# A graph network on one core: the sum by source reads its three bf16 parts in place

## The chip, the cores and the metric

The kernel runs on one core of a Trainium2 chip. The metric is the device time of one execution in microseconds (us), lower is better. The kernel before takes 10541.72 us, the median of 3 runs (10540.14 to 10548.04).

## The reference

Four graph layers are applied to 12,500 nodes with 64 features, over 212,500 edges, each with a layer norm before it and a residual after it. The stage that changes belongs to the first layer:

```python
msg = edge_val[:, None] * support[edge_col]
out = jax.ops.segment_sum(msg, edge_row, num_segments=x.shape[0])
```

The number of edges of each source node (its degree) is also needed by later layers, and is summed in the same stage as a 65th column of ones.

## The kernel before, in words

An earlier stage (`scatter_by_source`) has written one record of 131 fp32 words for each edge to HBM, sorted by the block of 128 nodes to which its source belongs: 64 words of message, a one, 64 words for a later layer, and two index words, of which one is the lane of the node in its block. The records fill 1760 tiles of 128. `sum_by_source` reads them back in 220 chunks of 8 tiles (`CB`), and sums each tile into its block with a matmul: the stationary operand is a one-hot matrix (record by lane) in bf16, the moving operand the messages. To keep fp32 precision with bf16 operands a message is split into three bf16 parts that stand side by side (`m.parts`: high, middle, low and a column of ones, 193 columns); the products go into three neighbouring stretches of a PSUM bank and are added at the end. Blocks take the 8 banks in turn.

For each chunk:

- SP (L925 to L933) waits until the chunk four before it has been consumed, loads 524 KB of records into one of 4 slots, reads the chunk's last block number, waits until the bank that this block needs has been emptied (`evacuated`), and gives TensorE `room`.
- GpSimd (POOL) casts the messages to bf16 (L946, high part), casts the remainder (L952, middle part), and subtracts (L954, low part). It issues L946 of chunk n before L952 and L954 of chunk n-1.
- VectorE (DVE) makes the 8 one-hot matrices in one instruction (L987, 1024 elements a partition) and subtracts the high part from the messages in place (L991, 512 elements).
- TensorE (PE) reads 8 bank offsets into registers, waits for `room`, `onehot` and `lo`, and issues 8 matmuls (L1012).

For each of the 98 blocks, ScalarE (ACT) copies 193 columns of the bank to `part_sums` once the block's tiles are summed (L1025) and clears the bank (L1027). After the last block, DVE and POOL share the blocks at 66 and add high, middle and low over all of them (L967, L970, L993, L997), and DVE takes the degree out (L994). The next stage, `columns_of`, begins with a POOL copy (L549).

No planner sets the order; each engine has its own list of instructions and semaphores tie them together. `settle` is a no-operation that an engine issues behind its waits. The last stage, `gather_by_source`, has two DVE instructions of nearly the same shapes (L1252, 512 elements, and L1255, 1024 elements), while POOL only issues DMAs.

Of the kernel before, what the change touches and what calls it, by code (L numbers as in the profile page):

```python
# [14 lines left out]
P = 128  # L15
N = 12500
E = 212500
D = 64
NB = -(-N // P)
# [15 lines left out]
TS = 1760  # L35
# [5 lines left out]
BODY = 160  # L41
BODIES = TS // BODY
CB = 8
PARTS = 3 * D + 2
NOWHERE = NP - 1
LOW = 1e30
TAIL = 32
# [4 lines left out]
BANK = 512  # L52
# [46 lines left out]
def allocate(nc, ctx):  # L99
# [23 lines left out]
    m.out_ring = arena[:, top + RING * D:top + RING * D + 2 * CH * REC]  # L123


    at = NB * PARTS
    m.part_sums = arena[:, 0:at].rearrange("p (b f) -> p b f", b=NB)
    m.rec_ring = arena[:, at:at + 4 * CB * REC]
    at += 4 * CB * REC
    m.parts = arena[:, at:at + 4 * CB * PARTS // 2].bitcast(BF16).rearrange("p (s f) -> p s f", f=PARTS)  # L130
    at += 4 * CB * PARTS // 2
    m.onehot16 = arena[:, at:at + 4 * CB * P // 2].bitcast(BF16).rearrange("p (c s f) -> p c s f", c=4, s=CB)
    assert at + 4 * CB * P // 2 <= top + 2 * NODE


    m.second_ring = arena[:, BOTH:BOTH + RING * RW]
# [520 lines left out]
def settle(engine):  # L657

    engine.nop(nofuse=True)  # L659
# [239 lines left out]
def sum_by_source(nc, m, sums):  # L899

    with ExitStack() as ctx:
        s = sems(nc, "blank", "hi", "rest", "mid", "lo", "onehot", "room", "summed", "copied", "evacuated", "halfway", "dst_in")
        rec_in = ring(nc, "rec_in", 4)
        block = ctx.enter_context(nc.Block())
        chunks = BODY // CB
        rows = 3 * D + 1
        bank_of = lambda b: slice(b % BANK_COUNT * BANK, b % BANK_COUNT * BANK + rows)
        records = m.sorted.rearrange("(p t) f -> p (t f)", p=P)
        rec = m.rec_ring.rearrange("p (s f) -> p s f", f=REC)
        tiles = lambda c: slice(c % 4 * CB, c % 4 * CB + CB)  # L910
        z = lambda c: rec[:, tiles(c), 0:D]
        part = lambda c, n: m.parts[:, tiles(c), n * D:(n + 1) * D]
        arrived = lambda i, c: i * (chunks // 4 * 16) + c // 4 * 16 + 16
        hi, mid, lo = (m.part_sums[:, :, n * D:(n + 1) * D] for n in range(3))
        whole = sums[:, :, 0:D]
        POOLS = 66

        @block.sync
        def _(sp):
            sp.dma_start(m.dst, m.dst_kept).then_inc(s["dst_in"], 16)  # L920
            with sp.Fori(0, BODIES) as i:
                for c in range(chunks):
                    n = i * chunks + c

                    sp.wait_ge(s["onehot"], n + 1)  # L925
                    sp.wait_ge(s["lo"], n + 1)
                    settle(sp)
                    sp.dma_start(m.rec_ring[:, c % 4 * CB * REC:(c % 4 + 1) * CB * REC],
                                 records[:, bass.ds(i * (BODY * REC) + c * (CB * REC), CB * REC)]).then_inc(rec_in[c % 4], 16)
# [6 lines left out]
        @block.gpsimd  # L936
        def _(pool):
            g = nc.gpsimd
            pool.sem_inc(s["lo"], 4)

            def first(i, c):

                pool.wait_ge(rec_in[c % 4], arrived(i, c))
                pool.wait_ge(s["summed"], i * BODY + c * CB + CB)
                settle(pool)
                g.tensor_copy(part(c, 0), z(c)).then_inc(s["hi"], 1)  # L946

            def others(i, c):
                n = i * chunks + c
                pool.wait_ge(s["rest"], n + 1)  # L950
                settle(pool)
# [4 lines left out]
            def body(i, lead):  # L956
                for c in range(chunks):
                    first(i, c)
                    if c or not lead:
                        others(i, c - 1)  # L960

            body(0, True)
            with pool.Fori(1, BODIES) as i:
                body(i, False)
            others(BODIES - 1, chunks - 1)
            pool.wait_ge(s["evacuated"], BANK_COUNT + NB)
            g.tensor_tensor(hi[:, POOLS:NB, :], hi[:, POOLS:NB, :], mid[:, POOLS:NB, :], ALU.add).then_inc(s["halfway"], 1)  # L967
            pool.wait_ge(s["halfway"], 2)
            pool.wait_ge(s["summed"], 4 * CB + TS)
            g.tensor_tensor(whole[:, POOLS:NB, :], hi[:, POOLS:NB, :], lo[:, POOLS:NB, :], ALU.add)  # L970

        @block.vector
        def _(dve):
            v = nc.vector
            v.memset(m.banks[:, :], 0.0).then_inc(s["blank"], 1)
            v.memset(m.parts[:, :, 3 * D:PARTS], 1.0).then_inc(s["blank"], 1)
            v.sem_inc(s["onehot"], 4)
            dve.wait_ge(s["blank"], 2)
            v.sem_inc(s["evacuated"], BANK_COUNT)

            with dve.Fori(0, BODIES) as i:
                for c in range(chunks):
                    n = i * chunks + c
                    dve.wait_ge(rec_in[c % 4], arrived(i, c))

                    dve.wait_ge(s["summed"], n * CB + CB)
                    v.tensor_tensor(m.onehot16[:, c % 4, :, :], m.iota_row[:, :].unsqueeze(1).to_broadcast([P, CB, P]),  # L987
                                    rec[:, tiles(c), REC_LANE:REC_LANE + 1].to_broadcast([P, CB, P]),
                                    ALU.is_equal).then_inc(s["onehot"], 1)
                    dve.wait_ge(s["hi"], n + 1)  # L990
                    v.tensor_tensor(z(c), z(c), part(c, 0), ALU.subtract).then_inc(s["rest"], 1)  # L991
            dve.wait_ge(s["evacuated"], BANK_COUNT + NB)
            v.tensor_tensor(hi[:, 0:POOLS, :], hi[:, 0:POOLS, :], mid[:, 0:POOLS, :], ALU.add).then_inc(s["halfway"], 1)  # L993
            v.tensor_copy(m.dout[:, :].unsqueeze(2), m.part_sums[:, :, 3 * D:3 * D + 1])  # L994
            dve.wait_ge(s["halfway"], 2)
            dve.wait_ge(s["summed"], 4 * CB + TS)
            v.tensor_tensor(whole[:, 0:POOLS, :], hi[:, 0:POOLS, :], lo[:, 0:POOLS, :], ALU.add)  # L997

        @block.tensor
        def _(pe):  # L1000
            pe.sem_inc(s["summed"], 4 * CB)
            with pe.Fori(0, BODIES) as i:
                for c in range(chunks):
                    n = i * chunks + c
                    banks = run_values(nc, ENG.PE, m.sorted_bank[0:1, bass.ds(n * CB, CB)], (BANK_COUNT - 1) * BANK)

                    pe.wait_ge(s["room"], n * CB + CB)
                    pe.wait_ge(s["onehot"], n + 1 + 4)
                    pe.wait_ge(s["lo"], n + 1 + 4)
                    settle(pe)  # L1010
                    for j in range(CB):
                        nc.tensor.matmul(m.banks[:, bass.ds(banks[j], rows)], m.onehot16[:, c % 4, j, :],  # L1012
                                         m.parts[:, c % 4 * CB + j, 0:rows],
                                         start=False, stop=False, skip_group_check=True).then_inc(s["summed"], 1)

        @block.scalar
        def _(act):
            a = nc.scalar
            for b in range(NB):
# [3 lines left out]
                act.wait_ge(s["summed"], ends[b % 8] + 4 * CB)  # L1023
                settle(act)
                a.activation(m.part_sums[:, b, 0:rows], m.banks[:, bank_of(b)], ACT.Copy).then_inc(s["copied"], 1)  # L1025
                act.wait_ge(s["copied"], b + 1)
                a.activation(m.banks[:, bank_of(b)], m.zero[:, 0:1].to_broadcast([P, rows]), ACT.Copy).then_inc(s["evacuated"], 1)  # L1027


def gather_by_tile(nc, m, a, layer):  # L1030
# [965 lines left out]
```

## Time and profile before

| | |
|---|---|
| median of 3 runs | 10541.72 us |
| the profiled execution | 10548.82 us |
| its span, first to last instruction | 10546.8 us |
| busy in the span: POOL, PE, DVE, ACT | 7448.4, 6987.8, 6022.0, 2062.7 us |
| mean granted TensorE clock | 0.524 of full speed |

A line of the profile's groups reads: line of the kernel, engine, operation, output<-inputs, shape, count, then busy time, mean duration in ns, and the idle time of the engine just before those instructions with what ended it. `PEld` is the weight load of TensorE, and a name such as `PEldq` or `SPq` is the engine's queue, where waits for semaphores show. The tensors that share the large buffer of this kernel all appear as `arena`.

### The profile page before, as it was taken

How to read it: one execution, taken by the hardware profiler on the slowest of the kernel's cores; microseconds unless marked ns; L12 is line 12 of the kernel's file. 1: busy time of each engine (PE TensorE's matmuls, PEld its weight loads, DVE VectorE, ACT ScalarE, POOL GpSimd, SP SyncE). 2: the span in 40 equal slices, each digit the busy share in tenths (PEclk: the TensorE clock that was granted, in tenths of full speed). 3: DMA queues.
4: the chain of work that ended last, by engine and by line, in shares of the span. 5: the costliest groups of instructions: out<-in, count | busy, mean ns of one | idle time of the engine just before them, and what ended most of it. 6: DMA issues, size and time to landing. Idle time of an engine off the chain costs nothing. (4 is left out here: it accounts for less than half of the span.)

```text
span 10546.8 us, 178097 instructions
## 1 busy us (share of the span) xinstructions
PE 6987.8 (66%) x25668; PEld 5267.0 (50%) x25669; DVE 6022.0 (57%) x22548; ACT 2062.7 (20%) x8089; POOL 7448.4 (71%) x7517
## 2 busy tenths in 40 slices
PE   0666766664443688888884555555566878787885
PEld 0555555553222566666663333333344656665664
DVE  5777777776887444444445555555554444444443
ACT  3244444442001000000000222222212111111112
POOL 0377777777998577777773777777754777777773
PEclk9555555555555555555555555555556555555556
DMA  5233333333443122222221222222211222222223
GB/s 90 68 105 105 105 105 105 105 105 102 149 147 110 52 55 53 53 53 53 53 55 34 53 53 53 55 53 53 53 35 54 77 77 76 79 77 77 76 77 29
DMA packets 441036, 783.01 MB, mean 74 GB/s; under 512 B 192009, under 2 KB 220329, under 8 KB 439854
## 3 DMA queue, kind: packets, MB, share of 16 engines
q1 hardware_dynamic: 223614, 494.23, 16.4%
q0 software_dynamic: 216064, 278.76, 11.2%
q14 instruction: 894, 7.32, 0.2%
q10 hardware_dynamic: 432, 2.16, 0.1%
q8 instruction: 32, 0.52, 0.0%
HBM read 634.79 MB, written 139.85 MB: 73 GB/s over the span
## 5 line engine op out<-in xcount | busy, mean ns | idle before, releaser
L1206 POOL DMA_INDIRECT arena<-node_table,idx x3328 | 3157.9, 949 | 1193.6 <-issue 742.1
L1151 PE MATMUL banks<-arena,onehot 128*128 x7040 | 2480.7, 471 | 1290.4 <-ACT arena L1192 561.2
L1151 PEld LDWEIGHTS banks<-arena,onehot 128*128 128x128 f32 x7040 | 1759.0, 312 | 1941.6 <-issue 1785.8
L1322 POOL DMA_INDIRECT arena<-node_table,arena x1760 | 1768.7, 1005 | 561.4 <-issue 429.1
L893 POOL DMA_INDIRECT sorted_edges<-arena,idx x1664 | 1634.6, 982 | 614.1 <-issue 575.1
L843 PE MATMUL banks<-arena,onehot 128*128 x3520 | 1116.9, 427 | 560.4 <-DVE onehot L792 546.9
L1104 DVE TENSOR_SCALAR onehot<-iota_row,block_base,edge_tables 128x128 f32<-128x128 f32 x3520 | 1253.7, 358 | 372.5 <-PE banks L1151 292.5
L1112 DVE TENSOR_TENSOR arena<-arena,banks 128x65 f32 (+1 forms) x3520 | 895.5, 254 | 909.6 <-PE banks L1151 892.7
L843 PEld LDWEIGHTS banks<-arena,onehot 128*128 128x128 f32 x3520 | 883.0, 314 | 786.1 <-issue 782.4
L1298 PE MATMUL banks<-arena 128*128 128x64 f32 x3520 | 1214.2, 448 | 0.0
L1293 PE MATMUL banks<-arena 128*64 128x65 f32 x3520 | 842.9, 343 | 481.7 <-ACT arena L1309 471.8
L1298 PEld LDWEIGHTS banks<-arena 128*128 128x128 f32 x3520 | 883.5, 311 | 210.5
L1100 DVE TENSOR_TENSOR arena<-arena 128x64 f32<-128x64 f32 x1664 | 382.7, 230 | 928.3 <-DMA arena<-node_table,idx 823.6
L1293 PEld LDWEIGHTS banks<-arena 128*64 128x64 f32 x3520 | 509.2, 206 | 724.7 <-ACT arena L1309 569.9
L1309 ACT ACTIVATE arena<-arena 128x64 f32<-128x64 f32 x1760 | 450.0, 257 | 1897.2 <-DVE arena L1263 1876.9
L1162 PE MATMUL banks<-arena 128*64 128x64 f32 x3328 | 791.2, 341 | 21.3 <-issue 13.1
L792 DVE TENSOR_SCALAR onehot<-arena,block_part 128x128 f32 x1760 | 555.6, 316 | 430.0 <-issue 403.4
L1263 DVE TENSOR_TENSOR arena<-arena 128x64 f32<-128x64 f32 x1760 | 403.3, 230 | 690.7 <-DMA arena<-node_table,arena 683.4
L868 ACT ACTIVATE arena<-arena,edge_tables 128x64 f32<-128x64 f32 x1664 | 510.7, 342 | 1321.8 <-DVE arena L802 956.5
L1192 ACT ACTIVATE arena<-arena 128x64 f32<-128x64 f32 x1664 | 426.2, 256 | 1670.8 <-DVE arena L1100 1669.6
L838 PE MATMUL banks<-w_pair,arena 128*128 128x128 f32 x1664 | 630.0, 482 | 129.7 <-ACT arena L873 91.9
L1012 PE MATMUL banks<-arena 128*128 128x193 bf16 x1760 | 323.8, 364 | 547.0 <-POOL arena L954 547.0
(289 smaller groups left out, 7038.5 us busy)
## 6 DMA issues: line engine op xcount, KB each, us to landing
arena<-sorted_edges SPq DMA_DIRECT2D x440, 524.0 KB, 3.5
arena<-in_attr_t SPq DMA_DIRECT2D x208, 512.0 KB, 3.5
arena<-row_keys SPq DMA_DIRECT2D x110, 512.0 KB, 4.9
arena<-in_attr_pairs SPq DMA_DIRECT2D x104, 512.0 KB
arena<-node_table,idx POOLq DMA_INDIRECT x3328, 2.4
arena<-node_table,arena POOLq DMA_INDIRECT x1760, 2.5
sorted_edges<-arena,idx POOLq DMA_INDIRECT x1664, 2.3
node_table<-arena SPq DMA_DIRECT2D x3, 3136.0 KB, 12.6
```

Of the source, the lines that this page charges most:

```text
L792: v.tensor_scalar(m.onehot[:, j % 4, :], m.row_ring[:, bass.ds(slots[j] * P, P)], m.block_part[:, bass.ds(blocks[j], 1)], None, ALU.is_equ ...
L838: nc.tensor.matmul(m.psum[4 + n % 4][:, 0:P], m.pair_ring[c % 2][:, n % 8 * P:(n % 8 + 1) * P], m.w_pair[:, :], start=True, stop=True).the ...
L843: nc.tensor.matmul(m.psum[j % 4][:, 0:D], m.onehot[:, j % 4, :], m.support[:, bass.ds(blocks[j] * D, D)], start=True, stop=True).then_inc( ...
L893: nc.gpsimd.indirect_dma_start(m.sorted, bass.IndirectOffsetOnAxis(ap=m.idx[:, j % (4 * CH):j % (4 * CH) + 1], axis=0), m.out_ring[:, slot ...
L1104: v.tensor_scalar(m.onehot[:, j % 4, :], m.iota_row[:, :], m.block_base[:, bass.ds(blocks[j], 1)], targets[:, bass.ds(tiles[j], 1)], ALU.a ...
L1112: v.tensor_tensor(rows, rows, m.psum[j % 4][:, 0:width], ALU.add).then_inc(s["added"], 1)
L1151: nc.tensor.matmul(to, m.onehot[:, j % 4, :], rows, start=True, stop=True).then_inc(s["summed"], 1)
L1162: done = nc.tensor.matmul(m.psum[GRAM][0:D, 0:D], attr, attr, start=False, stop=False, skip_group_check=True)
L1206: nc.gpsimd.indirect_dma_start(slot(j), None, m.table, bass.IndirectOffsetOnAxis(ap=m.idx[:, j:j + 1], axis=0)).then_inc(gathered[j % 32], 16)
L1293: nc.tensor.matmul(m.psum[GRAM][0:D, 0:RW], row[:, 0:D], row, start=False, stop=False, skip_group_check=True)
L1298: nc.tensor.matmul(m.psum[j % 4][:, 0:D], m.onehot8[:, c % 4, j % CB, :], row[:, 0:D], start=True, stop=True).then_inc(s["summed"], 1)
L1322: nc.gpsimd.indirect_dma_start(slots[:, j % SLOTS, 0:D], None, m.table, bass.IndirectOffsetOnAxis(ap=rec_i[:, j % SLOTS, REC_DST:REC], axis=0)
```

## The change

The three parts are no longer cast. The upper 16 bits of an fp32 word are a bf16 number, the word cut off after 8 bits of mantissa. The records land in the first of three rings of fp32 (`value(c, 0)`); DVE writes the remainder, the message less its upper half, to the second ring, and what remains of that to the third. The matmul reads the upper halves of the three rings in place, as a moving operand of 3 stretches of 65 bf16 elements with a step of two (195 columns, since each part now carries the column of ones or its remainder). Rings have 5 slots instead of 4 (`DEEP`), and SP waits for the matmuls of the chunk five before. POOL has no work per chunk. It adds each block's three parts right behind ScalarE's copy, into `sums`, and `part_sums` shrinks to 8 blocks, so that ScalarE also waits until POOL is done with the block eight before (`whole`). The additions behind the last block go.

```diff
-PARTS = 3 * D + 2
+DEEP = 5
...
+        rings = m.rings.rearrange("p (n s f) -> p n s f", n=3, f=REC)
+        upper = m.rings.bitcast(BF16).rearrange("p (n s f a) -> p n s f a", n=3, f=REC, a=2)
+        value = lambda c, n: rings[:, n, tiles(c), 0:RW]
+        part = lambda c, n: upper[:, n, tiles(c), 0:RW, 1]
...
-                    sp.wait_ge(s["onehot"], n + 1)
-                    sp.wait_ge(s["lo"], n + 1)
+                    sp.wait_ge(s["summed"], n * CB + CB)
...
-                g.tensor_copy(part(c, 0), z(c)).then_inc(s["hi"], 1)
...
-                g.tensor_copy(part(c, 1), z(c)).then_inc(s["mid"], 1)
-                pool.wait_ge(s["mid"], n + 1)
-                g.tensor_tensor(part(c, 2), z(c), part(c, 1), ALU.subtract).then_inc(s["lo"], 1)
...
-            g.tensor_tensor(whole[:, POOLS:NB, :], hi[:, POOLS:NB, :], lo[:, POOLS:NB, :], ALU.add)
...
-            v.memset(m.parts[:, :, 3 * D:PARTS], 1.0).then_inc(s["blank"], 1)
...
                     dve.wait_ge(s["summed"], n * CB + CB)
-                    v.tensor_tensor(m.onehot16[:, c % 4, :, :], ...
+                    v.tensor_tensor(value(c, 1), value(c, 0), part(c, 0), ALU.subtract).then_inc(s["rest"], 1)
+                    v.tensor_tensor(m.onehot16[:, c % DEEP, :, :], m.iota_row[:, :].unsqueeze(1).to_broadcast([P, CB, P]),
+                                    rings[:, 0, tiles(c), REC_LANE:REC_LANE + 1].to_broadcast([P, CB, P]),
                                     ALU.is_equal).then_inc(s["onehot"], 1)
-                    dve.wait_ge(s["hi"], n + 1)
-                    v.tensor_tensor(z(c), z(c), part(c, 0), ALU.subtract).then_inc(s["rest"], 1)
+                    dve.wait_ge(s["rest"], n + 2)
+                    v.tensor_tensor(value(c, 2), value(c, 1), part(c, 1), ALU.subtract).then_inc(s["lo"], 1)
...
                     for j in range(CB):
-                        nc.tensor.matmul(m.banks[:, bass.ds(banks[j], rows)], m.onehot16[:, c % 4, j, :],
-                                         m.parts[:, c % 4 * CB + j, 0:rows],
+                        parts = upper[:, :, c % DEEP * CB + j, 0:RW, 1]
+                        to = m.banks[:, bass.ds(banks[j], width)].rearrange("p (n f) -> p n f", n=3)
+                        nc.tensor.matmul(to, m.onehot16[:, c % DEEP, j, :], parts,
                                          start=False, stop=False, skip_group_check=True).then_inc(s["summed"], 1)
...
+                act.wait_ge(s["whole"], b + 1)
...
+        @block.gpsimd
+        def _(pool):
+            g = nc.gpsimd
+            for b in range(NB):
+                hi, mid, lo = (m.part_sums[:, b % BANK_COUNT, n * RW:(n + 1) * RW] for n in range(3))
+                pool.wait_ge(s["copied"], b + 1)
+                settle(pool)
+                g.tensor_tensor(sums[:, b, :], hi, mid, ALU.add).then_inc(s["halfway"], 1)
+                pool.wait_ge(s["halfway"], b + 1)
+                g.tensor_tensor(sums[:, b, :], sums[:, b, :], lo, ALU.add).then_inc(s["whole"], 1)
+            pool.wait_ge(s["whole"], BANK_COUNT + NB)
+            g.tensor_copy(m.dout[:, :].unsqueeze(2), sums[:, :, D:RW])
```

## Rows read from the trace of the kernel before

**Rows 1.** The page: the span and its busy time by engine

```profile
span 10546.8 us, 178097 instructions
PE 6987.8 (66%) x25668; PEld 5267.0 (50%) x25669; DVE 6022.0 (57%) x22548; ACT 2062.7 (20%) x8089; POOL 7448.4 (71%) x7517
```

**Rows 2.** Busy time by stretch: the stage's middle (length, engines, clock, DMA share, GB/s)

```profile
2600.00:3340.00 740.00, 300.05 (x1632) 207.55 (x1631) 637.11 (x409) 62.02 (x186) 723.49 (x612) 0.50 0.50 148
```

**Rows 3.** Timeline of one chunk in the middle (start us, duration us, engine, line)

```profile
2902.53 0.61 POOL L952 CAST arena<-arena 128x512 bf16<-128x512 f32 x1
2902.61 1.07 DVE L991 TENSOR_TENSOR arena<-arena 128x512 f32<-128x512 f32 x1 [0.50 <-POOL arena L946]
2903.22 1.44 POOL L954 TENSOR_TENSOR arena<-arena 128x512 bf16<-128x512 f32 x1
2903.60 2.14 DVE L987 TENSOR_TENSOR arena<-iota_row,arena 128x1024 bf16<-128x1024 f32 x1
2904.61 1.60 POOL L946 CAST arena<-arena 128x512 bf16<-128x512 f32 x1
...
2904.85 1.47 PE L1012 MATMUL banks<-arena 128*128 128x193 bf16 x8 [2.16 <-POOL arena L954]
2906.16 0.61 POOL L952 CAST arena<-arena 128x512 bf16<-128x512 f32 x1
```

**Rows 4.** Timeline of the stage's first chunks

```profile
2567.68 1.23 DVE L987 TENSOR_TENSOR arena<-iota_row,arena 128x1024 bf16<-128x1024 f32 x1 [1.38 <-DMA arena<-sorted_edges]
...
2569.41 0.69 DVE L991 TENSOR_TENSOR arena<-arena 128x512 f32<-128x512 f32 x1 [0.50 <-POOL arena L946]
...
2573.47 1.81 DVE L987 TENSOR_TENSOR arena<-iota_row,arena 128x1024 bf16<-128x1024 f32 x1 [0.25 <-DMA arena<-sorted_edges]
```

**Rows 5.** Timeline of the last stage, DVE, where POOL computes nothing

```profile
9006.35 0.69 DVE L1252 TENSOR_TENSOR arena<-arena,scale_row 128x512 f32<-128x512 f32 x1 [0.62 <-issue]
9006.96 1.22 DVE L1255 TENSOR_TENSOR arena<-iota_row,arena 128x1024 f32<-128x1024 f32 x1
9008.10 0.22 DVE L1263 TENSOR_TENSOR arena<-arena 128x64 f32<-128x64 f32 x1
```

**Rows 6.** Timeline of the stage's end

```profile
3364.77 5.48 DVE L993 TENSOR_TENSOR arena<-arena 128x4224 f32<-128x4224 f32 x1
3365.77 4.94 POOL L952 CAST arena<-arena 128x512 bf16<-128x512 f32 x1
...
3371.87 4.54 POOL L967 TENSOR_TENSOR arena<-arena 128x2048 f32<-128x2048 f32 x1
...
3372.11 1.47 PE L1012 MATMUL banks<-arena 128*128 128x193 bf16 x8 [4.62 <-POOL arena L954]
...
3376.49 8.90 POOL L970 TENSOR_TENSOR arena<-arena 128x2048 f32<-128x2048 f32 x1
3386.09 0.93 POOL L549 COPY arena<-arena 128x896 f32 x1 [0.71 <-DVEq L1402]
```

**Rows 7.** Waits of the queues at semaphores (ns min/median/max), 2900 to 2911 us

```profile
L659 SPq EVENT_SEMAPHORE  x4: 2181/2182/2187, 2898.9 to 2909.8; - x4
L659 PEldq EVENT_SEMAPHORE  x4: 1670/1702/1706, 2899.4 to 2910.3; - x4
```

**Rows 8.** Other instructions used as bounds: groups by shape, and one timeline line

```profile
L1780 POOL TENSOR_SCALAR_AFFINE_SELECT valid<-valid 128x1 f32<-128x1 f32 x1 | 0.2, 187 | 32.4 <-SPq L1740 32.4
...
L1298 PE MATMUL banks<-arena 128*128 128x64 f32 x3520 | 1214.2, 448 | 0.0
...
L1012 PE MATMUL banks<-arena 128*128 128x193 bf16 x1760 | 323.8, 364 | 547.0 <-POOL arena L954 547.0
...
3475.12 1.73 PE L595 MATMUL banks<-w_l,arena 128*128 128x128 f32 x14
```

**Rows 9.** Busy time by stretch: the first record loads, and fp32 matmuls

```profile
2570.00:2572.00 2.00, 0.00 (x0) 0.00 (x0) 1.33 (x2) 0.00 (x0) 1.55 (x1) 0.50 0.87 270
...
3474.00:3480.00 6.00, 6.00 (x57) 6.00 (x56) 3.63 (x6) 2.32 (x5) 1.98 (x3) 1.00 0.00 0
```

**Rows 10.** Record loads, 2562 to 3386 us: issue, and us to landing; ScalarE's copies

```profile
arena<-sorted_edges SPq DMA_DIRECT2D x220, 524.0 KB, 3.5
...
L1025 ACT ACTIVATE arena<-banks 128x193 f32<-128x193 f32 x98 | 32.6, 333 | 769.0 <-PE banks L1012 769.0
```

More of the change, by code:

```diff
@@ L123, in allocate @@
     m.out_ring = arena[:, top + RING * D:top + RING * D + 2 * CH * REC]
[L126 to L133, printed above, removed]
+    at = BANK_COUNT * 3 * RW
+    m.part_sums = arena[:, 0:at].rearrange("p (b f) -> p b f", b=BANK_COUNT)
+    m.rings = arena[:, at:at + 3 * DEEP * CB * REC]
+    at += 3 * DEEP * CB * REC
+    m.onehot16 = arena[:, at:at + DEEP * CB * P // 2].bitcast(BF16).rearrange("p (c s f) -> p c s f", c=DEEP, s=CB)
+    assert at + DEEP * CB * P // 2 <= top + NODE
     m.second_ring = arena[:, BOTH:BOTH + RING * RW]
@@ L901, in sum_by_source @@
     with ExitStack() as ctx:
-        s = sems(nc, "blank", "hi", "rest", "mid", "lo", "onehot", "room", "summed", "copied", "evacuated", "halfway", "dst_in")
-        rec_in = ring(nc, "rec_in", 4)
+        s = sems(nc, "blank", "rest", "lo", "onehot", "room", "summed", "copied", "evacuated", "halfway", "whole", "dst_in")
+        rec_in = ring(nc, "rec_in", DEEP)
         block = ctx.enter_context(nc.Block())
         chunks = BODY // CB
-        rows = 3 * D + 1
-        bank_of = lambda b: slice(b % BANK_COUNT * BANK, b % BANK_COUNT * BANK + rows)
+        width = 3 * RW
+        early = DEEP * CB
+        bank_of = lambda b: slice(b % BANK_COUNT * BANK, b % BANK_COUNT * BANK + width)
         records = m.sorted.rearrange("(p t) f -> p (t f)", p=P)
[L909 to L916, printed above, removed]
+        rings = m.rings.rearrange("p (n s f) -> p n s f", n=3, f=REC)
+        upper = m.rings.bitcast(BF16).rearrange("p (n s f a) -> p n s f a", n=3, f=REC, a=2)
+        tiles = lambda c: slice(c % DEEP * CB, c % DEEP * CB + CB)
+        value = lambda c, n: rings[:, n, tiles(c), 0:RW]
+        part = lambda c, n: upper[:, n, tiles(c), 0:RW, 1]
+        arrived = lambda i, c: i * (chunks // DEEP * 16) + c // DEEP * 16 + 16
         @block.sync
@@ L934, in _ @@
             sp.wait_ge(s["dst_in"], 16)
[L936 to L945, printed above, removed]
-                g.tensor_copy(part(c, 0), z(c)).then_inc(s["hi"], 1)
[L948 to L951, printed above, removed]
-                g.tensor_copy(part(c, 1), z(c)).then_inc(s["mid"], 1)
-                pool.wait_ge(s["mid"], n + 1)
-                g.tensor_tensor(part(c, 2), z(c), part(c, 1), ALU.subtract).then_inc(s["lo"], 1)
[L956 to L969, printed above, removed]
-            g.tensor_tensor(whole[:, POOLS:NB, :], hi[:, POOLS:NB, :], lo[:, POOLS:NB, :], ALU.add)
         @block.vector
@@ L975, in _ @@
             v.memset(m.banks[:, :], 0.0).then_inc(s["blank"], 1)
-            v.memset(m.parts[:, :, 3 * D:PARTS], 1.0).then_inc(s["blank"], 1)
-            v.sem_inc(s["onehot"], 4)
-            dve.wait_ge(s["blank"], 2)
+            v.sem_inc(s["rest"], 1)
+            dve.wait_ge(s["blank"], 1)
             v.sem_inc(s["evacuated"], BANK_COUNT)
@@ L983, in _ @@
                     n = i * chunks + c
-                    dve.wait_ge(rec_in[c % 4], arrived(i, c))
+                    dve.wait_ge(rec_in[c % DEEP], arrived(i, c))
                     dve.wait_ge(s["summed"], n * CB + CB)
-                    v.tensor_tensor(m.onehot16[:, c % 4, :, :], m.iota_row[:, :].unsqueeze(1).to_broadcast([P, CB, P]),
-                                    rec[:, tiles(c), REC_LANE:REC_LANE + 1].to_broadcast([P, CB, P]),
+                    v.tensor_tensor(value(c, 1), value(c, 0), part(c, 0), ALU.subtract).then_inc(s["rest"], 1)
+                    v.tensor_tensor(m.onehot16[:, c % DEEP, :, :], m.iota_row[:, :].unsqueeze(1).to_broadcast([P, CB, P]),
+                                    rings[:, 0, tiles(c), REC_LANE:REC_LANE + 1].to_broadcast([P, CB, P]),
                                     ALU.is_equal).then_inc(s["onehot"], 1)
-                    dve.wait_ge(s["hi"], n + 1)
-                    v.tensor_tensor(z(c), z(c), part(c, 0), ALU.subtract).then_inc(s["rest"], 1)
[L992 to L997, printed above, removed]
+                    dve.wait_ge(s["rest"], n + 2)
+                    v.tensor_tensor(value(c, 2), value(c, 1), part(c, 1), ALU.subtract).then_inc(s["lo"], 1)
         @block.tensor
         def _(pe):
-            pe.sem_inc(s["summed"], 4 * CB)
+            pe.sem_inc(s["summed"], early)
             with pe.Fori(0, BODIES) as i:
@@ L1018, in _ @@
             a = nc.scalar
+            act.sem_inc(s["whole"], BANK_COUNT)
             for b in range(NB):
@@ L1021, in _ @@
                     ends = bounded_values(nc, ENG.Activation, m.tiles_upto[0:1, b:min(b + 8, NB)], TS)
-                act.wait_ge(s["summed"], ends[b % 8] + 4 * CB)
+                act.wait_ge(s["summed"], ends[b % 8] + early)
+                act.wait_ge(s["whole"], b + 1)
                 settle(act)
-                a.activation(m.part_sums[:, b, 0:rows], m.banks[:, bank_of(b)], ACT.Copy).then_inc(s["copied"], 1)
+                a.activation(m.part_sums[:, b % BANK_COUNT, :], m.banks[:, bank_of(b)], ACT.Copy).then_inc(s["copied"], 1)
                 act.wait_ge(s["copied"], b + 1)
-                a.activation(m.banks[:, bank_of(b)], m.zero[:, 0:1].to_broadcast([P, rows]), ACT.Copy).then_inc(s["evacuated"], 1)
+                a.activation(m.banks[:, bank_of(b)], m.zero[:, 0:1].to_broadcast([P, width]), ACT.Copy).then_inc(s["evacuated"], 1)
+        @block.gpsimd
[10 more added lines that the diff above has]
+            g.tensor_copy(m.dout[:, :].unsqueeze(2), sums[:, :, D:RW])
 def gather_by_tile(nc, m, a, layer):
```

8 lines of the change are left out of this document (4 added, 4 removed).

## The prediction

> **What bounds the kernel now.** I read the page first: POOL is the busiest engine of the whole span, but only at 71% [rows 1], so an average says nothing of this stage. The stretches then show the changed stage alone: in its middle, 740 us long, POOL is busy 723 us, DVE 637, PE 300, and the DMA engines half the time [rows 2]. One would say: POOL bounds it. The timeline of one chunk says more. The period, from one L952 to the next, is 2906.16 - 2902.53 = 3.63 us [rows 3]. The reader should look at the durations. L991 takes 1.07 us there, but 0.69 in the stage's first chunk, where POOL stood still [rows 4]. L987 takes 2.14 us, but 1.23 for the very first one [rows 4], and the same shape takes 1.22 in the last stage [rows 5]. L946 and L952 are the same cast, at 1.60 and 0.61 us. The ends fit together: L954 ends at 2904.66, and L987, which had started at 2903.60, ends 1.07 us after that, just 1024 elements at the 1.04 ns that the slope between L1252 and L1255 gives ((1.22 - 0.69) / 512). L946 starts at 2904.61 and ends 0.47 us after L987's end at 2905.74. At the stage's end L952 takes 4.94 us because it stands behind L993 [rows 6]. So DVE's two-input instructions and POOL's take turns; none of them advances while the other has the turn. The 3.63 us are the sum of the two engines' work: about 0.47 and 0.47 (casts), 0.99 (L954), 0.53 and 1.07 (DVE), and small gaps. What bounds the stage is the pair POOL and DVE together, and work that goes from POOL to DVE is worth its difference in duration, not its removal from a busier engine.
>
> **The change, part by part.** *DVE per chunk.* It now issues a subtraction of 520 elements, the one-hot of 1024, and a second subtraction of 520. With POOL silent the price is start to start, from the last stage: L1252 to L1255 0.61 us, L1255 to the next 1.14 us [rows 5]. Eight more elements add 0.01, and this one-hot's bf16 output 0.01 (1.23 against 1.22). The sum is 0.62 + 1.15 + 0.62 = 2.39 us a chunk, 220 x 2.39 = 525.8 us. The second subtraction waits for the first, but the one-hot lies between, so nothing is exposed. If no overlap of the next start were left, the durations add to 0.70 + 1.23 + 0.70 = 2.63, 53 us more over the stage; that is the upper end. The in-place operand (bf16, step of two) has no row here; L991 mixes fp32 and bf16 too, at 0.69, the same as fp32 alone (L1252), so I take no extra.
>
> *PE.* Its queue waits 1.70 us of every 3.63 [rows 7], so a chunk costs it 1.93 us: the eight matmuls and the register reads. 195 columns for 193 add 0.01. It fits under 2.39 with 0.45 to spare, and every matmul's wait is then for the second subtraction. The strided moving operand has no row either. From below it costs nothing. From above I take the fp32 stream: 14 matmuls of 128 columns in 1.73 us [rows 8] at the full granted clock [rows 9], 0.12 us each, so 0.25 at the half clock of this stage, 0.38 for 195 columns against (1.47 - 0.37) / 7 = 0.16 now, 0.37 being the time of the last one (L1012's mean [rows 8]). I take nothing, since the array is fed the same bf16 columns, and keep the other end as a rival below.
> The Trainium skill, "SBUF — State Buffer", in the section "SBUF: two separate sides", says that a read may step within a 16-byte line at full rate, up to 8 bf16 elements; by it the step of two is free. No row here shows a strided bf16 matmul.
>
> *SP and DMA.* SP waits 2.18 us of each period [rows 7], so its loop needs 1.45 us: it fits. A load is issued when the matmuls of the chunk five before are done, some 1.7 us behind that chunk's last subtraction; the landing takes 3.5 us [rows 10] and DVE needs it four periods, 9.6 us, after that subtraction. 4 us are left. The loads would need 148 x 3.63 / 2.39 = 225 GB/s; the first loads reached 270 at a share of 0.87 [rows 9]. Hidden.
>
> *The first chunks.* Loads arrive late there: the third one-hot starts at 2573.47, 5.79 us after the first [rows 4], where DVE would now be ready after 2 x 2.39. That costs 1.0 us. The removed memset is worth 0.1.
>
> *POOL and ACT per block.* Each of 98 blocks brings two POOL additions of 65 elements, and each takes the turn from DVE. L967 has 2.2 ns per element [rows 6], so 0.14 us of it, of which 0.08 was DVE's start anyway: 0.06 is the low end. The high end is a whole short POOL instruction, 0.19 (L1780 [rows 8]) with 0.14 on it, less the overlap: 0.25. I take 0.10, nearer the low end because L954 held DVE for its elements alone. 196 x 0.10 = 20 us (12 to 49). POOL waits for DVE in turn, at most about 1.2 us per addition, against 98 blocks in some 540 us, 5.5 us each, with 8 buffers: ACT's new wait and, behind it, `evacuated`, `room` and PE are not delayed. ACT's two instructions cost 0.33 us each [rows 10].
> The Trainium skill, "GPSIMD Engine Reference", section "Engine selection", says to put two-input elementwise work on VectorE, GpSimd being about half as fast. The rows agree on the speed (2.2 ns against 1.04), but by that rule the additions would be 196 DVE instructions at the 0.22 us of L1263 [rows 5], 43 us, where POOL's cost 20 on the same path: the rule is against this placement by speed, and I expect the row's price to win.
>
> *The tail.* Today the last matmuls start at 3372.11, the end additions run until 3385.39 [rows 6]. Now the stage ends with the matmuls of the last chunk, 1.8 us behind the last subtraction (0.2 to start, 1.5, and a little). The last block's copy is over before: nothing is left for POOL but a copy of 98 elements.
>
> *Sum.* Before, from the first one-hot at 2567.68 to 3385.39: 817.7 us. After: 525.8 + 1.0 - 0.1 + 20 + 1.8 = 548.5. The gain is 269 us. Against the profiled execution (10548.8, its span being 10546.8) this gives 10280; the median of the runs is 7 us below that execution, so 10541.7 - 269 = 10273 us.
>
> **The rivals.** *TensorE reads the strided parts at the fp32 stream's pace.* Then a chunk costs PE 1.93 + 8 x (0.38 - 0.16) = 3.69 us, and 220 of them 812 us, against 799 now. With the tail and POOL's end additions gone (12 us) and no turns on the path, this is a draw: 10541.7 - 817.7 + 812 + 1 + 2 = 10539. Against it: an fp32 product needs more of the array than a bf16 one, and 0.25 us for 128 columns is well over what the bf16 stream takes. A half-way case (0.27 a matmul) gives 2.81 a chunk and 10345.
> *Slower than before, by the same place at a higher price:* from 0.38 us a matmul TensorE decides against the change. With the longest narrow fp32 matmul, 0.45 (L1298 [rows 8]), a chunk takes 1.93 + 8 x 0.29 = 4.25 us, 220 of them 935 us, so 10662. For it: the operand is now picked out of 4-byte words in three far stretches. Against: nothing in the rows ties price to address.
> *DVE needs two cycles for an element of the halves in place:* 520 x 1.04 = 0.54 more per subtraction, 3.47 us a chunk, 238 us more: 10511. L991's unchanged price with one bf16 operand speaks against it, though that one was dense.
> *POOL never gets its turn while DVE's train is unbroken.* Then PE runs out of banks after 16 blocks, DVE stops, and POOL catches up, some 5 us each time, at most 12 times: 60 us instead of 20, so 10313. Against: L954 got the turn between L991 and L987 although L987 had been issued before L991 ended [rows 3].
> *The pair was not the bound but POOL alone:* then DVE was never slowed by POOL, and its rows of 1.07 and 2.14 hold. 1.07 + 2.14 + 1.07 = 4.28 us a chunk would be slower (10689). The first chunk's rows exclude it.
>
> **How the numbers follow.** The forecast with its own bounds holds 0.80, POOL's starvation 0.05 (also faster), DVE at two cycles 0.04 (faster), a half-way TensorE 0.04 (faster), the draw 0.02, slower 0.05 for the priced case and its relatives. So faster by over 0.2% (21 us, about what a measurement of this kernel can tell from no change) 0.93, within 0.02, slower 0.05. The lower bound is DVE at 2.36 a chunk (-7) and the additions at the low end or hidden (-20): 10245. The upper takes 2.63 a chunk (+53) and the dear additions (+29): 10355. The range, which also holds the starved POOL and nearly the half-way TensorE, is 10240 to 10360.
>
> **What the changed profile would show.** The first subtraction and the second at 0.70 us and the one-hot at 1.23, back to back on a DVE busy nearly all the time; a period of 2.39 to 2.5; POOL's additions at up to 1.4 us, most of it waiting for the turn, and a DVE instruction behind each lengthened by about 0.1; PE waiting for the second subtraction, its eight matmuls still 1.47 long; the next stage's L549 copy about 269 us earlier; all later stages unmoved. Subtractions of 1.2 us, matmuls over 0.2 apart, or waits of DVE for loads or for `summed` would make the prediction wrong.

## The result, and the profile after

The changed kernel takes 10268.22 us, the median of 4 runs (10257.39 to 10270.65), against 10541.15 before: a ratio of 0.9738, 95% interval 0.9723 to 0.9753. The forecast was 10273, the range 10240 to 10360. A later set, 5 runs beside 9 of the kernel before, gave 0.9739 (0.9726 to 0.9752).

The page's first lines, of the changed kernel, answer to [rows 1]:

```profile
span 10268.8 us, 177022 instructions
PE 6995.5 (68%) x25668; PEld 5260.8 (51%) x25669; DVE 5863.1 (57%) x22764; ACT 2061.8 (20%) x8089; POOL 6848.6 (67%) x7052
```

The busy time by stretch, of the changed stage's middle, answers to [rows 2] (length, PE, PEld, DVE, ACT, POOL, clock, DMA share, GB/s):

```profile
2600.00:3080.00 480.00, 288.14 (x1552) 194.71 (x1552) 474.74 (x583) 59.17 (x178) 190.73 (x178) 0.50 0.74 217
```

DVE is now busy 474.7 of 480 us. The clock did not move. POOL still shows 190.7 us, for 178 instructions of 65 elements: 76.8 us of it are a single one (below), the other 177 take 0.65 us in the mean. The timeline of the changed kernel, one chunk without POOL and the start of one with it, answers to [rows 3]:

```profile
2841.16 0.69 DVE L951 TENSOR_TENSOR arena<-arena 128x520 f32<-128x520 f32 x1
...
2841.77 0.69 DVE L946 TENSOR_TENSOR arena<-arena 128x520 f32<-128x520 f32 x1
...
2842.04 1.49 PE L968 MATMUL banks<-arena 128*128 128x195 bf16 x8 [1.08 <-DVE arena L951]
2842.38 1.21 DVE L947 TENSOR_TENSOR arena<-iota_row,arena 128x1024 bf16<-128x1024 f32 x1
...
2843.51 0.69 DVE L951 TENSOR_TENSOR arena<-arena 128x520 f32<-128x520 f32 x1
...
2843.96 0.40 POOL L993 TENSOR_TENSOR arena<-arena 128x65 f32<-128x65 f32 x1 [3.81 <-ACT arena L982]
2844.12 0.79 DVE L946 TENSOR_TENSOR arena<-arena 128x520 f32<-128x520 f32 x1
```

L951 (the second subtraction) to L951 is 2.35 us. L946, L947 and L951 last 0.69, 1.21 and 0.69 us and each starts some 0.08 before the last one ends. The eight matmuls take 1.49 us for 195 strided columns, 1.47 for 193 dense ones before. Where POOL starts an addition inside L951, POOL ends 0.16 us after L951 does, and the next DVE instruction is 0.10 longer.

There is one thing that no row of before had. The timeline of the changed kernel around the only long instruction of POOL:

```profile
2603.59 76.79 POOL L993 TENSOR_TENSOR arena<-arena 128x65 f32<-128x65 f32 x1 [5.18 <-ACT arena L982]
...
2679.53 0.69 DVE L951 TENSOR_TENSOR arena<-arena 128x520 f32<-128x520 f32 x1
...
2680.46 0.32 POOL L995 TENSOR_TENSOR arena<-arena 128x65 f32<-128x65 f32 x1
...
2680.86 0.34 ACT L982 ACTIVATE arena<-banks 128x195 f32<-128x195 f32 x1 [41.05 <-POOL arena L995]
...
2681.93 1.49 PE L968 MATMUL banks<-arena 128*128 128x195 bf16 x8 [2.39 <-SPq L929]
...
2685.44 0.70 DVE L946 TENSOR_TENSOR arena<-arena 128x520 f32<-128x520 f32 x1 [5.22 <-DMA arena<-sorted_edges]
```

One addition of 65 elements takes 76.8 us, and ends when DVE stops. Read upwards: ScalarE had waited 41 us for it, since `part_sums` has room for 8 blocks; so no bank was emptied, SP gave no `room`, PE stopped, no load was issued, and DVE stood still for 5.2 us. POOL then caught up with 16 additions of 0.3 us.

The last rows of the changed stage (timeline) answer to [rows 6]:

```profile
3106.46 0.69 DVE L951 TENSOR_TENSOR arena<-arena 128x520 f32<-128x520 f32 x1
...
3107.34 1.49 PE L968 MATMUL banks<-arena 128*128 128x195 bf16 x8 [0.87 <-DVE arena L951]
3109.53 1.81 POOL L547 COPY arena<-arena 128x896 f32 x2 [13.50 <-DVEq L1372]
```

From DVE's memset of the PSUM banks at its start to the next stage's first POOL copy the stage took 3386.09 - 2562.71 = 823.4 us before (the copy in [rows 6]) and 3109.53 - 2557.67 = 551.9 now: 271.5 us less, of 278.0 by the spans. The other 6.5 lie in front of the stage (5.0) and behind it, in code that the change does not touch. By the medians of the runs the gain is 272.9 us.

### The profile page after: what moved, and what is told of

Same layout as the page of the kernel before. It is cut to its first block and busy times, and to the rows that moved or that the text cites. A ratio compares the mean times of both kernels' runs of the same rounds, so it can differ in the third digit from the quotient of the medians.

```text
span 10268.8 us, 177022 instructions
## 1 busy us (share of the span) xinstructions
PE 6995.5 (68%) x25668; PEld 5260.8 (51%) x25669; DVE 5863.1 (57%) x22764; ACT 2061.8 (20%) x8089; POOL 6848.6 (67%) x7052
## 5 line engine op out<-in xcount | busy, mean ns | idle before, releaser
L1263 PEld LDWEIGHTS banks<-arena 128*64 128x64 f32 x3520 | 508.9, 205 | 723.6 <-ACT arena L1279 574.4
L790 DVE TENSOR_SCALAR onehot<-arena,block_part 128x128 f32 x1760 | 551.9, 314 | 427.1 <-issue 396.7
L1132 PEld LDWEIGHTS banks<-arena 128*64 128x64 f32 x3328 | 480.4, 205 | 225.8 <-issue 35.4
```

The costliest lines, as they stand in the source:

```text
L790: v.tensor_scalar(m.onehot[:, j % 4, :], m.row_ring[:, bass.ds(slots[j] * P, P)], m.block_part[:, bass.ds(blocks[j], 1)], None, ALU.is_equ ...
L1132: done = nc.tensor.matmul(m.psum[GRAM][0:D, 0:D], attr, attr, start=False, stop=False, skip_group_check=True)
L1263: nc.tensor.matmul(m.psum[GRAM][0:D, 0:RW], row[:, 0:D], row, start=False, stop=False, skip_group_check=True)
```

## The experiments

The first two sets of runs took place on two other chips, on which each kernel takes some 40% longer. On chip 5, with the kernel before at 14719 us, ran the second profile of the changed kernel, the one without additions and the two with more work for POOL; on chip 6, with 14723 us, the small one-hot, the four slots, the one-hot in eight and the first run of the parts summed in PSUM. The third set (chip 13, kernel before 10544 us) has the rest. The three other stages that issue indirect DMAs are slower on the first two chips (3480 us against 2135 for the one in front), the changed stage is not. So whole times are told beside the kernel before on the same chip, and the stage by itself. The small one-hot, the two kernels with more work for POOL, and the gap were run only once.

```
kernel                          stage, us                       length  additions over 70 us
before                          2562.71 to 3386.09               823.4  -
changed                         2557.67 to 3109.53               551.9  1
changed, second profile         3901.05 to 4460.05               559.0  3
changed, third profile          2555.73 to 3110.98               555.3  2
no additions                    3911.21 to 4437.68               526.5  -
POOL reads more                 3903.51 to 4663.40               759.9  1
POOL writes more                3900.97 to 4453.83               552.9  1
before, small one-hot           3897.46 to 4518.20               620.7  -
four slots                      3901.86 to 4460.37               558.5  3
one-hot in eight                3900.55 to 4475.30               574.8  0
parts summed in PSUM            3909.74 to 4436.19               526.5  -
parts summed in PSUM, again     2544.28 to 3070.78               526.5  -
paired one-hot                  2545.27 to 2997.25               452.0  -
gap in DVE's train              2557.71 to 3136.94               579.2  0
```

**The changed kernel again**, with no edit.

> The changed kernel as it is, for a narrower interval and a second profile. Turn theory (POOL's reading instructions and DVE's two-input instructions exclude each other): median 10262 to 10272, DVE back to back at 2.36 us a chunk without POOL, and of POOL's 196 additions none, one or two that wait over 10 us because DVE's train has no gap; each such wait costs one stop of DVE of about 5 us. Rival, that the 76.8 us of the one addition in the first profile is an error of that record: no stop of DVE in this profile and no addition over 2 us.

Measured: 14448.84 us (14444.3 to 14469.74), 270 less than before on that chip (0.9822, 0.9808 to 0.9835); the median that was expected belongs to the faster chip and was not tested. The profile has three additions over 70 us, one more than the most expected. The long wait is no fault of one record: it comes with a stop of DVE each time, 18.2 us of idle time before L946 in all (1.7 of it in the first chunks).

The same kernel once more, in the last set:

> The changed kernel once more, as the base for the other two: one to three additions of 70 to 77 us in its profile, each with one stop of DVE of about 5 us; the stage, from DVE's first memset to the next stage's first POOL copy, 548 us plus 3.5 us for each stop.

Measured: 10268.95 us, two long additions, the stage 555.3. The timeline of this third profile, POOL alone:

```profile
2844.44 74.43 POOL L993 TENSOR_TENSOR arena<-arena 128x65 f32<-128x65 f32 x1 [5.18 <-ACT arena L982]
...
2953.90 76.78 POOL L993 TENSOR_TENSOR arena<-arena 128x65 f32<-128x65 f32 x1 [5.18 <-ACT arena L982]
```

Three profiles, with 1, 2 and 3 stops, give 551.9, 555.3 and 559.0: a stage of 548.4 and 3.5 a stop (5.2 idle, less the additions that then cost DVE nothing).

The long waits do not fall at random. Over six profiles (those of the table with a count of 1 to 3) there are eleven, and they belong to the additions of only four blocks: the first, seventh, 52nd and 72nd of the 98. All eleven begin 0.59 to 0.62 us after the start of a one-hot. In these profiles 60 additions begin at that point; the other 49 ended some 0.16 us after that same one-hot.

**Is the before-kernel's bound the pair, or POOL?** The kernel before, with the one-hot for one tile of eight.

```diff
-v.tensor_tensor(m.onehot16[:, c % 4, :, :], m.iota_row[:, :].unsqueeze(1).to_broadcast([P, CB, P]),
-                rec[:, tiles(c), REC_LANE:REC_LANE + 1].to_broadcast([P, CB, P]),
+v.tensor_tensor(m.onehot16[:, c % 4, 0:1, :], m.iota_row[:, :].unsqueeze(1).to_broadcast([P, 1, P]),
+                rec[:, c % 4 * CB:c % 4 * CB + 1, REC_LANE:REC_LANE + 1].to_broadcast([P, 1, P]),
```

> The kernel BEFORE, with its one-hot made for one tile of eight only (the other seven stay zero and their messages are lost). POOL's work is untouched. Turn theory: the period of 3.63 us holds 0.93 us of this DVE instruction (896 elements x 1.04 ns), so it falls to about 2.7 us and the time by 200 us. Rival, that POOL alone bounds the kernel before (busy 723 of 740 us): the same time as before, since POOL's instructions stay.

Measured: 14502.96 us against 14723.33, 220 less, and the stage 202.7 less. Its timeline:

```profile
4200.77 0.70 DVE L988 TENSOR_TENSOR arena<-iota_row,arena 128x128 bf16<-128x128 f32 x1 [0.42 <-DMA arena<-sorted_edges]
4201.26 0.68 POOL L946 CAST arena<-arena 128x512 bf16<-128x512 f32 x1
...
4201.88 0.61 POOL L952 CAST arena<-arena 128x512 bf16<-128x512 f32 x1
...
4202.57 1.45 POOL L954 TENSOR_TENSOR arena<-arena 128x512 bf16<-128x512 f32 x1
4203.44 0.72 DVE L988 TENSOR_TENSOR arena<-iota_row,arena 128x128 bf16<-128x128 f32 x1 [0.40 <-DMA arena<-sorted_edges]
```

POOL's instructions are the same, yet the cast L946 takes 0.68 us where it took 1.60 [rows 3], and the period is 2.70 in the mean. (Of the 220 us that the one whole time shows, 18 lie outside the stage and are not explained; a wait of DVE for each load, 0.4 us, is new, and POOL does not stand still for it.) So POOL's busy share was for a good part waiting for DVE. The theory that POOL alone was the bound is gone.

**POOL reads more, POOL writes more.** One more two-input addition of 1024 elements per block on scratch, and in the other kernel two memsets of 1024 elements.

```diff
+g.tensor_tensor(scratch[:, 2048:3072], scratch[:, 0:1024], scratch[:, 1024:2048], ALU.add)
```

```diff
+g.memset(scratch[:, 2048:3072], 0.0)
+g.memset(scratch[:, 1024:2048], 0.0)
```

> The changed kernel with one more POOL instruction per block, a two-input addition of 1024 elements on scratch. POOL would still be idle more than half the time. Turn theory: each of 98 holds DVE for its elements, 1024 x 2.14 ns = 2.19 us less the 0.08 of DVE's start, 98 x 2.11 = 207 us: about 10475. Rival (DVE and POOL do not exclude each other, POOL is only slow by itself): the same time, 10268.

> As the kernel with the extra POOL addition, but with two memsets of 1024 elements per block instead, which write and read nothing. If only what POOL reads takes the turn from DVE (as the Trainium skill, SBUF - State Buffer, section Who interferes with whom, says): 10268, no DVE instruction longer than beside the additions. If any use of SBUF by POOL takes the turn: two memsets at about 1.07 us each hold DVE for 98 x 2.0 = 196 us, about 10465.

Measured: 14690.75 and 14447.29 us, one run each, beside 14448.84 for the changed kernel. The stage with the addition is 208.0 us longer than that of the changed kernel with as many stops (759.9 against 551.9), by 207 expected; with the memsets it is 1.0 us longer. By the whole times the addition costs 242 us, some 40 of them outside the stage and not explained. The timeline with the addition:

```profile
4304.41 0.79 DVE L947 TENSOR_TENSOR arena<-arena 128x520 f32<-128x520 f32 x1
4304.61 2.80 POOL L1001 TENSOR_TENSOR arena<-arena 128x1024 f32<-128x1024 f32 x1
...
4305.13 3.37 DVE L948 TENSOR_TENSOR arena<-iota_row,arena 128x1024 bf16<-128x1024 f32 x1
```

The one-hot (L948 in this kernel) takes 3.37 us in place of 1.21, and ends 1.09 us after POOL's addition. The groups by shape of the kernel with the memsets:

```profile
L948 DVE TENSOR_TENSOR arena<-iota_row,arena 128x1024 bf16<-128x1024 f32 x220 | 272.6, 1239 | 0.0
...
L1002 POOL MEMSET arena<- 128x1024 f32 x98 | 93.0, 949 | 0.0
```

POOL's memsets take 0.95 us each beside DVE and leave the one-hot at 1.24, as with no memsets. In these two kernels only what POOL reads takes the turn. That agrees with the Trainium skill, "SBUF — State Buffer", section "Who interferes with whom": a DVE instruction with two SBUF inputs contends with a GpSimd instruction that reads SBUF, not with one that only writes.

**What POOL's additions cost.** They are left out; the sums stay zero.

```diff
-g.tensor_tensor(sums[:, b, :], hi, mid, ALU.add).then_inc(s["halfway"], 1)
-pool.wait_ge(s["halfway"], b + 1)
-g.tensor_tensor(sums[:, b, :], sums[:, b, :], lo, ALU.add).then_inc(s["whole"], 1)
+pool.sem_inc(s["whole"], 1)
```

> Leaves out the addition of the three parts: POOL only passes the semaphore on (the sums stay zero). Turn theory: 180 additions that run beside DVE at 0.11 us each (20 us) and the one stop of DVE (5 us) go, so the stage is 25 us shorter and the time about 10243; all DVE instructions at 0.69 and 1.21 us. Rival, that POOL's small additions cost DVE nothing and the period is set by DVE's own overheads: same time as the changed kernel, 10268.

Measured: 14432.73 us, 16 less than the changed kernel on that chip (25 were expected; its stage begins 10 us later, for no reason that the record shows), and a stage of 526.5: 25.4 less than the first profile of the changed kernel, 21.9 less than its stage without a stop. 21.9 / 196 = 0.112 us an addition. The stage's middle, DVE's groups by shape, in this kernel:

```profile
L947 DVE TENSOR_TENSOR arena<-iota_row,arena 128x1024 bf16<-128x1024 f32 x191 | 230.3, 1206 | 0.0
L946 DVE TENSOR_TENSOR arena<-arena 128x520 f32<-128x520 f32 x192 | 130.9, 682 | 0.0
```

**Do the five slots matter?** `DEEP = 4` in place of 5.

> The changed kernel with rings of 4 slots instead of 5. A load then is issued three periods (7.1 us) less 1.9 us before DVE needs it, and landings took 3.5 to 5 us: 0 to 1.5 us to spare. If that holds, the same time as the changed kernel (270 us less than before). If landings take over 5 us where the DMA engines are busy three quarters of the time, DVE waits for loads, some 0.3 to 1 us a chunk: 70 to 220 us longer than the changed kernel.

Measured: a stage of 558.5 us with three long additions, against 559.0 for five slots with three. The loads have time enough with four. The whole time was 14480.38 (14466.5 to 14485.12), 243 less than the kernel before on the same chip, where 270 had been expected. The 27 us do not lie in this stage. The changed kernel was not run on this chip, so they say nothing of the slots.

**Can DVE's one-hot be cheaper?** Eight instructions of one input and a scalar per partition.

```diff
+for j in range(CB):
+    made = v.tensor_scalar(m.onehot16[:, c % DEEP, j, :], m.iota16[:, :],
+                           rings[:, 0, c % DEEP * CB + j, REC_LANE:REC_LANE + 1], None, ALU.is_equal)
+made.then_inc(s["onehot"], 1)
```

> The changed kernel with the one-hot of a chunk made by 8 instructions of one input (bf16 row of lanes, compared with a scalar per partition, bf16 out) in place of one of two inputs. DVE bounds the changed stage at 2.36 us a chunk, of which the one-hot has 1.14. If one such instruction takes 0.13 us start to start (as L1263 to L1270 in the rows of before, 64 elements): 1.04, so 2.26 us a chunk, 22 us faster than the changed kernel. If each takes 0.2: 2.8 us a chunk and about 100 us slower. If the queue in front of TensorE (1.93 us a chunk) becomes the bound, not under 1.95 us a chunk: at best 90 us faster.

Measured: 14485.94 us, 237 less than the kernel before on that chip, and a stage of 574.8, 26 more than the changed kernel's without a stop. Its timeline:

```profile
4200.25 1.38 DVE L950 TENSOR_SCALAR arena<-iota,arena 128x128 bf16<-128x128 bf16 x8
4201.55 0.69 DVE L954 TENSOR_TENSOR arena<-arena 128x520 f32<-128x520 f32 x1
...
4203.37 0.33 POOL L996 TENSOR_TENSOR arena<-arena 128x65 f32<-128x65 f32 x1 [5.12 <-ACT arena L985]
```

Eight of them take 1.30 us start to start, 0.16 each, against 1.14 for the one instruction: between the two prices expected, and on the wrong side. The trace also shows something on the turns: 104 of POOL's 196 additions lie wholly beside these one-input instructions, and take 0.30 to 0.35 us, nearly as when DVE stood still. No addition of this kernel takes over 1.54 us, so there is no stop.

**The parts summed in PSUM.** Three matmuls of 65 columns on the same 65 columns of the bank; ScalarE copies them straight into `sums`.

```diff
-nc.tensor.matmul(to, m.onehot16[:, c % DEEP, j, :], parts, ...).then_inc(s["summed"], 1)
+for k in range(3):
+    done = nc.tensor.matmul(m.banks[:, bass.ds(banks[j], RW)], m.onehot16[:, c % DEEP, j, :],
+                            upper[:, k, c % DEEP * CB + j, 0:RW, 1],
+                            start=False, stop=False, skip_group_check=True)
+done.then_inc(s["summed"], 1)
```

> The changed kernel with the three parts summed in PSUM: three matmuls of 65 columns per tile onto the same 65 columns, ScalarE copies the block straight into the sums, POOL adds nothing. If weight loads are hidden as now, 24 matmuls at about 0.07 us fit in the period, POOL's turns (20 us) and DVE's stops (5 us each) go, and the stage is 25 us shorter than that of the changed kernel. If each matmul costs at least its weight load, 0.11 to 0.13 us, TensorE takes 24 x 0.12 + 0.67 = 3.6 us a chunk and is the bound: all of the gain is lost, the time is that of before.

> The kernel that sums the parts in PSUM, once more beside the paired one-hot: stage of 526 us as before; time 15 to 30 us under the changed kernel's.

Measured: 14433.4 us on chip 6, 290 less than the kernel before there, and 10229.39 on chip 13 (0.9701, 0.9688 to 0.9714), 39.6 under the changed kernel beside it, more than the 15 to 30 expected. Both stages are 526.5 us, just that of the kernel that leaves the additions out. By the profiles 28.8 of it are the stage and 11.4 lie in front of it, where the earlier stage's 1664 indirect DMAs took 958 ns in place of 967 (medians). Its timeline:

```profile
2799.64 0.72 DVE L946 TENSOR_TENSOR arena<-arena 128x520 f32<-128x520 f32 x1
2799.95 1.50 PE L967 MATMUL banks<-arena 128*128 128x65 bf16 x24 [0.86 <-DVE arena L951]
2800.25 1.25 DVE L947 TENSOR_TENSOR arena<-iota_row,arena 128x1024 bf16<-128x1024 f32 x1
```

24 matmuls take 1.50 us, the time of the 8 wide ones, which stream the same 1560 columns: 0.055 each, half of what I feared the weight load to cost.

**The paired one-hot**, on top of that. The one-hot is laid out so that two tiles alternate, and both inputs are packed bf16.

```diff
+v.tensor_copy(m.lanes16[:, c % DEEP, :], upper[:, 0, tiles(c), REC_LANE, 1]).then_inc(s["lanes"], 1)
...
+v.tensor_tensor(pairs[:, c % DEEP, :, :, :],
+                m.iota_pairs[:, :, :].unsqueeze(1).to_broadcast([P, CB // 2, P, 2]),
+                m.lanes16[:, c % DEEP, :].rearrange("p (g a) -> p g a", a=2).unsqueeze(2).to_broadcast([P, CB // 2, P, 2]),
+                ALU.is_equal).then_inc(s["onehot"], 1)
...
+nc.tensor.matmul(m.banks[:, bass.ds(banks[j], RW)], pairs[:, c % DEEP, j // 2, :, j % 2], ...)
```

> The kernel that sums the parts in PSUM, with the one-hot laid out in pairs of tiles so that both its inputs are packed bf16 (lanes copied to bf16 first, 8 elements). If DVE then makes two elements a cycle, the one-hot takes 0.60 us start to start instead of 1.14, the copy adds about 0.1, and a chunk takes 0.61 + 0.60 + 0.61 + 0.1 = 1.93 us; TensorE's queue needs 1.93 and the loads 1.75, so 1.95 to 2.05 us a chunk and 65 to 90 us less than the kernel that sums in PSUM. If the rate does not change, the copy makes it 20 us longer. If TensorE reads the one-hot, now with a step of two, at half rate, it becomes the bound: over 2.4 us a chunk, longer by 10 us or more.

Measured: 10156.49 us (10152.45 to 10158.75; 0.9632, 0.9619 to 0.9645), 112 under the changed kernel and 73 under the one that sums in PSUM; the stage is 452.0. It is the fastest version of all. Its timeline:

```profile
2802.18 1.50 PE L974 MATMUL banks<-arena 128*128 128x65 bf16 x24 [0.48 <-DVE arena L953]
2802.24 0.17 DVE L950 COPY lanes<-arena 128x8 bf16<-128x8 bf16 x1
2802.32 0.70 DVE L951 TENSOR_TENSOR arena<-arena 128x520 f32<-128x520 f32 x1
2802.93 0.69 DVE L953 TENSOR_TENSOR arena<-iota_pairs,lanes 128x1024 bf16<-128x1024 bf16 x1
2803.53 0.70 DVE L958 TENSOR_TENSOR arena<-arena 128x520 f32<-128x520 f32 x1
```

1024 elements now take 0.69 us where they took 1.21. With the fixed part of the slope between L1252 and L1255 taken off (0.16), that is half a nanosecond for each, in place of 1.04. The train is 1.90 us a chunk where nothing waits, 2.02 in the mean; DVE now also waits for matmuls (9.4 us, 27 times) and loads (5.5 us, 16 times), which move 266 GB/s at a share of 0.85 from 2560 to 2980 us. TensorE's clock is not the same either: the granted clock of that stretch is 0.57, with PE busy 299 of 420 us, in place of 0.50 with 288 of 480. It is at full speed (2.4 GHz) for short stretches, in which 24 matmuls take 1.08 us, and at half of it in between. What this is worth was not tested.

**A gap in DVE's train.** On the changed kernel, DVE waits for its second subtraction before the next chunk's first.

```diff
+dve.wait_ge(s["lo"], n + 1)
 v.tensor_tensor(value(c, 1), value(c, 0), part(c, 0), ALU.subtract).then_inc(s["rest"], 1)
```

> The changed kernel, in which DVE also waits for the end of its last subtraction before the next chunk's first, so that its train has a gap once a chunk. If POOL's rare long waits come from a train without a gap: no addition of POOL takes over 2.5 us and DVE never stops for loads in the steady part; the gap costs 0.08 to 0.15 us a chunk, 18 to 33 us, of which the absent stops give back 4 us each. Rival, that the long waits have nothing to do with gaps: one to three additions of over 70 us again.

Measured: 10297.74 us, and a stage of 579.2, 30.8 more than that of the changed kernel without a stop: 0.14 a chunk. POOL's two additions in it (ns min/median/max):

```profile
L995 POOL TENSOR_TENSOR arena<-arena x98: 296/592/925, 2571.5 to 3120.5; 128x65 f32<-128x65 f32 x98
...
L997 POOL TENSOR_TENSOR arena<-arena x98: 633/659/757, 2572.5 to 3121.1; 128x65 f32<-128x65 f32 x98
```

None takes over 0.93 us. That fits the theory that the long waits need a train without a gap, but weakly: one profile, in which 8 additions begin 0.61 to 0.62 us after the start of a one-hot, and elsewhere only 11 of 60 such additions were long. That eight in a row are spared by chance is a rival left open. The gap costs more than the stops that it would prevent.

## Why the prediction was right, point by point

**The bound.** That DVE and POOL take turns, and that the 3.63 us are the sum of both, was read from durations that stretched. Both experiments on it came out at the expected size: 203 us less for a smaller DVE instruction with POOL untouched, 208 more for POOL reads with DVE untouched.

**DVE per chunk.** Forecast 2.39 us from start to start in another stage; measured 2.357 (the stage without additions: L946 starts from 3916.3 to 4432.9, 516.6 us, less 0.35 for two waits for loads, over 219 periods). 220 chunks cost 519 in place of 526. The subtraction reads the strided half in place at its old price, 0.68 to 0.69 us for 520 elements.

**PE.** Taken at no extra cost: 1.49 us for eight, 0.16 apart, the bound of 0.38 from the fp32 stream was over twice too high. PE waits for L951 each time, as forecast.

**SP, loads, first chunks.** Hidden, even with four slots. The first chunks cost 0.2 us, not 1.0: all that DVE waits between them is 0.19 us.

**POOL's additions.** 0.10 us each was taken, 0.112 measured, 22 us in place of 20. What I had wrong is the sentence that ScalarE's new wait delays nothing. POOL's waits were bounded at 1.2 us; one to three in 196 last 74 to 77. The rival "POOL never gets its turn" described the chain that follows and its 5 us a stop, but it was put as always or never. It is rare, and cost 3.5 to 10.6 us. DVE's cheaper train paid for it: that is luck, not foresight.

**The tail.** 1.8 us forecast, 3108.83 - 3107.15 = 1.7 measured.

**The sum.** By the bounds that the forecast used, from DVE's first instruction to the end of the last matmul, the stage takes 3108.83 - 2563.05 = 545.8 us where 548.5 were forecast: some 7 less for DVE's chunks and 1 less for the first ones, 2 more for the additions and 3.5 more for the one stop. The gain in the stage is then 271.9 us, 269 forecast. The range was also said to hold the half-way TensorE "nearly"; at 10345 it holds it fully.

The advice of the Trainium skill against elementwise work on GpSimd ("GPSIMD Engine Reference", section "Engine selection") was weighed at 43 us on DVE against 20 beside it. Measured on POOL were 22 us and the stops. The additions on DVE were not tried, so which engine is the better place is not shown; the best answer of those tried was to have neither do them.

## What to carry to other kernels

Where two engines are both busy most of a stage, compare one instruction's duration where the other engine is idle with its duration in the steady state; if it stretches by just the other's remaining time, the two take turns, and the price of work is the same on either but for speed. Take the instructions that read off the second engine before all else: 196 memsets on POOL cost DVE 1.0 us here, 98 additions of the same size 208. And where an accumulator can add the parts, try that first: summed in PSUM the stage took the 526.5 us of the kernel that adds nothing.

## What the runs showed of the hardware that was not expected

- A reading POOL instruction can wait for DVE far longer than one DVE instruction: 74.4 or 76.8 us in each of eleven cases over six profiles, until DVE stopped. The one in the first profile started 0.59 us into L947; eleven other additions of that profile started 0.59 to 0.60 into L947 as well and ended 0.77 to 0.78 us later. What decides it is open. How long such a wait lasts is set by the kernel: by when ScalarE, PE and the loads have run out of room and DVE stops. The one reading copy at the end of the train took 12.8 to 12.9 us with the parts summed in PSUM (L989) and without the additions, until DVE's last instruction.
- A bf16 moving operand with a step of two costs TensorE nothing (1.49 us for eight of 195 columns), nor does a stationary one (1.50 for 24 in both layouts, at a granted clock of 0.50); 24 narrow matmuls with a weight load each take as long as 8 wide ones with the same number of columns in all.
- With the 24 narrow matmuls DVE's instructions read longer (medians 0.72 and 1.25 us, on chip 6 0.83 and 1.35, against 0.68 and 1.21), yet their starts are as far apart as before, 2.36 us a chunk.
- The indirect DMAs of the stage in front took 972 (before), 971 and 967 (two profiles of the changed kernel) and 958 ns (parts summed in PSUM), by the medians, with the same code there: up to 18 us of the whole time. The cause is open, and so is that of the 14.7 ms on the two other chips.
